# Sums of squares of the Mamba scan's grouped norm, with the ones as stationary side

## The chip, the cores and the metric

The kernel runs on one core of one Trainium2 chip. The metric is the time of one execution on the device, in microseconds (us). Before the change the median of three runs is 2793.15 us, from 2792.43 to 2793.49.

## The reference

The whole program is four transformer-like layers in a row on a tensor x of 2 x 1024 x 256 in f32. The change touches only the third layer's attention part, a Mamba block with 32 heads of 64, 8 groups and a state of 32. Its end is what matters here: the output y of the scan is gated, normed in 8 groups of 256 channels by the root of the mean of squares, and projected.

```python
states = lax.associative_scan(combine, (a, db), axis=1)[1]
y = jnp.einsum('blhps,blhs->blhp', states, Ch) + D_param[None, None, :, None] * x
y = y.reshape(Bb, Ll, D_SSM) * jax.nn.silu(z)
yg = y.reshape(Bb, Ll, G, D_SSM // G)
var = jnp.mean(yg * yg, axis=-1, keepdims=True)
y = (yg * lax.rsqrt(var + EPS)).reshape(Bb, Ll, D_SSM) * norm_w
return y @ W_out + b_out
```

## The kernel before

The program runs as stages on one core; each engine (TensorE, ACT, DVE, POOL and the SyncE queue) has its own ordered list of instructions, and semaphores tie them. The stage of the change is `MambaScan` (classes `Mamba` and `MambaSteps` hold its buffers and its preparation). It goes over 32 steps n: two batches of 1024 tokens, 8 groups g of four heads (256 channels), and two halves of 512 tokens (`c4`), so n = 16 b + 2 g + c4. Channels lie on partitions and tokens on columns; the 256 channels of a group are two tiles of 128 partitions.

What one step does, by the names of its pieces:
- "raw" (TensorE L1771, evicted by ACT L1893, first tap on POOL L2062), taps on DVE (L1967) and "silu" (ACT L1900) make the convolved input; each pair of steps needs two tiles of 1024 tokens, made ahead. Each tile takes two raw products of 512 columns.
- "scan" (TensorE L1784, DVE L1974), "xd" (transposes L1792, DVE L1981), "bd" (DVE L2002), "cb" (TensorE L1805, ACT L1913, DVE L2009, POOL L2076), "cp" (TensorE L1797, DVE L1995), "st" (TensorE L1824), "h" (DVE L2022), "within" (TensorE L1840) and "across" (TensorE L1857) are the chunked scan.
- "end" (DVE L2031, two of them) adds D x and takes y out of PSUM; "gate" (TensorE L1812, ACT L1920) makes silu(z), and POOL L2082 multiplies y by it, two tiles.
- "square" (ACT L1929, two, then POOL L2086) squares both tiles and adds them; "var" (TensorE L1864) sums over the partitions; "mean" (ACT L1935) adds eps to a 1/256 of it, and POOL L2090 raises it to the power -1/2.
- "out" (TensorE L1874, two halves r = 0, 1) multiplies y by W_out, ACT L1945 evicts it with that power as its scale, and POOL L2098 adds it to x.

In "var" each chunk of 128 tokens is the stationary side and two columns of ones the moving side, so the sums come out with tokens on partitions, one column (twice) for each of four chunks, 128 x 8 in all. That is the form in which ACT needs a scale for "out", whose rows are tokens.

The order of the pieces on each engine is written by hand. `AT` gives each kind of piece, for each engine, a place relative to n; `order` sorts all pieces by n plus place, and each engine works through its list strictly in that order. On POOL, "mean" of step n stands at n+1.42, ahead of "cb" of step n+2 (n+1.5) and of "gate" of step n+1 (n+1.55 and n+1.6). On TensorE, behind "var" of an odd n comes "across" of n+1 (n+1.6); behind that of an even n, up to 26, come two "raw" products (n+1.5) and then "across". Three of the odd steps (3, 11, 19) also have raw products there.

Each engine counts its pieces done in one semaphore (`self.products`, `self.activations`, `self.results`, `self.pooled`), so to wait for a piece is to wait for all ahead of it in that engine's list. POOL's raw piece also waits for the first "end" of the step whose input buffer it writes over, which for the tile made behind an even n is step n+1.

PSUM banks are dealt out in rings. Ring A has two banks and serves, in TensorE's order, "raw", "gate", "var" and "out"; `take` makes TensorE wait until ACT has done the piece that reads what the bank held last. For "var" that piece is "mean", for the others the eviction of the same name. ACT's "out" waits for POOL's "mean":

```python
w.wait_ge(self.products, self.pn[step])
w.wait_ge(self.pooled, self.gn["mean", n])
```

Of the kernel before, what the change touches and what calls it, by code (L numbers as in the profile page):

```python
# [1620 lines left out]
class MambaScan(Stage):  # L1621
# [8 lines left out]
    AT = {  # L1630
        "pe": {"raw": (-2.5, -2), "scan": (-1.1, -1, -0.8, -0.6), "xd": (-0.75, -0.6), "cp": (-0.2,),
             "cb": (-0.74,), "st": (0.05,), "within": (0.25,), "across": (0.6,), "gate": (0.15, 0.3), "var": (1.45,),
             "out": (1.85, 2.2)},
        "act": {"raw": (-2.45, -2), "silu": (-1.4, -1.2), "cb": (-0.5,), "gate": (0.15, 0.35),
             "square": (1.05, 1.1), "mean": (1.45,), "out": (1.95, 2.2)},
# [3 lines left out]
        "pool": {"raw": (-2.45, -2.2), "sel": (-1.1,), "cb": (-0.5,), "gate": (0.55, 0.6), "square": (1.15,),  # L1639
             "mean": (1.42,), "out": (1.85, 2.35)},  # L1640
    }


# [4 lines left out]
    def __init__(self, net, mem, norm, clear):  # L1648
        self.net, self.m, self.norm, self.clear = net, mem, norm, clear
        conv, half = self.conv, self.half = [], []  # L1650
        for q in range(4):
            t = (8 * q, .0) if q == 0 else (8 * q, -1.0)
            conv += [(t, q // 2, 16 + q % 2, 0), (t, q // 2, 18 + q % 2, 1)]
        for u in range(16):
            conv += [((2 * u, 0.0), u // 8, 2 * (u % 8) + s, s) for s in range(2)]
        p, a, d, g = [self.order(k) for k in ("pe", "act", "dve", "pool")]
        self.orders = {"pe": p, "act": a, "dve": d, "pool": g}
        self.raws = [s[1:3] for s in p if s[0] == "raw" and s[3] == 0]
        self.raw = {r: i for i, r in enumerate(self.raws)}
        beside = [k for kinds in self.NORM.values() for k in kinds]  # L1660
        self.pn, self.an, self.dn, self.gn = [{s: i + 1 for i, s in enumerate(s for s in o if s[0] not in beside)}
                                              for o in (p, a, d, g)]

        ring_a, ring_b = Slots(2), Slots(3)
        self.slot = {}
        for step in p:
            if step[0] in ("raw", "gate", "var", "out"):
                self.slot[step] = ring_a.take("a", ("mean", step[1]) if step[0] == "var" else step)
            elif step[0] in ("bt", "cb"):
                self.slot[step] = ring_b.take("a", step)  # L1670
            elif step[0] in ("scan", "xd", "cp"):
                self.slot[step] = ring_b.take("d", step)
        self.products = net.flag("m_products", len(self.pn))
        self.activations = net.flag("m_activations", len(self.an))
        self.results = net.flag("m_dve_results", len(self.dn))
        self.pooled = net.flag("m_pool_results", len(self.gn))
        self.crep = [net.flag("m_crep%d" % i, 64 * 16) for i in range(2)]
        self.blank = net.flag("m_blank", 1)
# [78 lines left out]
    def pe(self, e, w):  # L1757
# [3 lines left out]
        for step in self.orders["pe"]:  # L1761
# [81 lines left out]
            elif kind == "across":  # L1843
                w.wait_ge(self.results, self.dn["cp", n])
                w.wait_ge(self.results, self.dn["h", n, 2])
                for i in range(4):
                    c = 4 * c4 + i
                    if c == 0:
                        continue
                    o = slice(c * 128, c * 128 + 128)  # L1850
                    v = slice(i * 128, i * 128 + 128)
                    w.wait_ge(self.results, self.dn[("h", n, i - 1) if i else ("h", n - 1, 3)])
                    H = m.H[self.state(n, i - 1) % 4]
                    for h in range(4):
                        q = slice(32 * h, 32 * h + 32)
                        r = slice(64 * (h % 2), 64 * (h % 2) + 64)
                        t = e.matmul(net.PS[r, self.Y[h // 2], v], H[q, :], m.CP[q, o], start=False, stop=True,  # L1857
                                     skip_group_check=True)
                t.then_inc(P.sem, 1)
            elif kind == "var":  # L1860
                p = self.take(w, step, self.A)
                w.wait_ge(self.pooled, self.gn["square", n])
                for i in range(4):
                    t = e.matmul(p[:, 2 * i:2 * i + 2], m.sq[0][:, i * 128:i * 128 + 128], net.ones[:, 0:2], start=True,  # L1864
                                 stop=True)
                t.then_inc(P.sem, 1)
            elif kind == "out":
                p = self.take(w, step, self.A)
                w.wait_ge(self.pooled, self.gn["gate", n, 0])
                w.wait_ge(self.pooled, self.gn["gate", n, 1])  # L1870
                for j in range(2):
                    c = c4 * 512 + (2 * step[2] + j) * 128
                    for k in range(2):
                        t = e.matmul(p[:, j * 256:j * 256 + 256], m.Y[:, k, c:c + 128], m.Wout[:, 2 * g + k, :],  # L1874
                                     start=(k == 0), stop=(k == 1))
                t.then_inc(P.sem, 1)
            elif kind == "turn":
                w.wait_ge(self.results, self.dn["end", self.N - 1, 1])
                w.wait_ge(self.results, self.dn["h", self.N - 1, 2])
                self.norm.pe_turn(e, w, n)  # L1880

    def act(self, e, w):
        net, m, A = self.net, self.m, self.activations
        for step in self.orders["act"]:
# [37 lines left out]
            elif kind == "square":  # L1922
# [1 line left out]
                c4 = n % 2  # L1924
                w.wait_ge(self.pooled, self.gn["gate", n, s])
                if n > 0:
                    w.wait_ge(self.products, self.pn["var", n - 1])
                    w.wait_ge(self.pooled, self.gn["square", n - 1])
                e.activation(m.sq[s], m.Y[:, s, c4 * 512:c4 * 512 + 512], ACT.Square).then_inc(A.sem, 1)  # L1929
            elif kind == "mean":  # L1930
                w.wait_ge(self.products, self.pn["var", n])
                if n > 1:
                    w.wait_ge(A, self.an["out", n - 2, 0])
                    w.wait_ge(A, self.an["out", n - 2, 1])
                e.activation(m.rs[n % 2], self.bank(("var", n), self.A)[:, 0:8], ACT.Identity, scale=1.0 / 256.0,  # L1935
                             bias=net.eps).then_inc(A.sem, 1)
            elif kind == "out":
                r = step[2]
                p = self.bank(step, self.A)
# [3 lines left out]
                    w.wait_ge(self.pooled, self.gn["out", n - 1, r])  # L1943
                for j in range(2):
                    t = e.activation(m.O[r][:, j * 256:j * 256 + 256], p[:, j * 256:j * 256 + 256], ACT.Copy,  # L1945
                                     scale=m.rs[n % 2][:, 2 * (2 * r + j):2 * (2 * r + j) + 1])
                t.then_inc(A.sem, 1)
            elif kind == "xnt":
                self.wait_read(w)
# [93 lines left out]
    def pool(self, e, w):  # L2043
        net, m, G = self.net, self.m, self.pooled
        e.memset(m.RAW[:, :, 0:3], 0.0).then_inc(self.blank.sem, 1)
        for step in self.orders["pool"]:
# [40 lines left out]
            elif kind == "mean":  # L2087
                r = m.rs[n % 2]
                w.wait_ge(self.activations, self.an[step])
                e.tensor_tensor(r, r, m.mhalf, ALU.pow).then_inc(G.sem, 1)  # L2090
            elif kind == "out":
                b, g, c4 = self.where(n)
                i = b * 8 + c4 * 4 + 2 * step[2]
# [1047 lines left out]
```

## Time and profile before

| | |
|---|---|
| median of three runs | 2793.15 us |
| span of the profiled execution | 2813.6 us |
| instructions in the trace | 35158 |
| TensorE, busy in the span | 2635.8 us, 94% |
| DVE | 1672.5 us, 59% |
| ACT | 1069.7 us, 38% |
| POOL | 945.6 us, 34% |
| mean granted clock of TensorE | 0.968 |
| "var" products | 1884.7 to 2461.1 us, 256 passes |

The profile is of one execution. Its lines name a line of the kernel, an engine, an operation, the written and read tiles, shape and count, and in square brackets how long the engine stood idle before it and what released it. TensorE's time is given in two rows, PE for the products and PEld for the loads of the stationary side, which overlap. Products are pipelined and their ends are modelled, so the start of the next group tells better than the printed length how long a group held the engine. The granted clock is a share of TensorE's full speed: 1.00 is 2.4 GHz and 0.50 is 1.2 GHz.

### The profile page before, as it was taken

What the parts mean: (1) busy time and instruction counts of PE and PEld (TensorE: products, weight loads), DVE (VectorE), ACT (ScalarE), POOL (GpSimd) and SP (SyncE); (2) the same over time, 40 slices, a digit from 0 to 9 for tenths busy, and PEclk for the clock granted to TensorE, in tenths of its full rate; (3) what the DMA queues carried; (4) which work ended last, traced back from release to release, by engine and by line L of the source; (5) the groups of instructions that cost most, each with busy time, mean ns of one, the idle gap of its engine ahead of it and who ended that gap; (6) DMA issues with size and microseconds to landing.
All of it is one profiled execution on the core that took longest, in us unless ns stands there. A gap on an engine that the chain in (4) does not pass through costs nothing. (4 is left out here: it accounts for less than half of the span.)

```text
span 2813.6 us, 35158 instructions
## 1 busy us (share of the span) xinstructions
PE 2635.8 (94%) x13426; PEld 1672.0 (59%) x13426; DVE 1672.5 (59%) x3408; ACT 1069.7 (38%) x1954; POOL 945.6 (34%) x921
## 2 busy tenths in 40 slices
PE   7988989999999999999999997889999999967996
PEld 4445544564656655566565565646666666635896
DVE  6676671228576574665752325579888888743333
ACT  2534552114454443534543113434444444322222
POOL 3221210004232232322320005336766766751122
PEclk8999999999999999999999999989999999968998
DMA  5222111026000000000001000000000000070123
GB/s 187 61 61 69 54 46 61 0 73 76 1 1 1 1 1 1 1 1 1 16 1 71 33 0 30 1 20 12 16 16 12 16 12 16 9 287 25 57 72 133
DMA packets 57112, 109.11 MB, mean 39 GB/s; under 512 B 13792, under 2 KB 32480, under 8 KB 55792
## 3 DMA queue, kind: packets, MB, share of 16 engines
q1 hardware_dynamic: 53152, 96.47, 11.8%
q0 software_dynamic: 3792, 10.39, 1.0%
q8 instruction: 107, 1.75, 0.3%
q14 instruction: 61, 0.50, 0.1%
HBM read 71.16 MB, written 27.08 MB: 35 GB/s over the span
## 5 line engine op out<-in xcount | busy, mean ns | idle before, releaser
L1256 PE MATMUL ps<-back 128*128 128x512 f32 x576 | 292.0, 596 | 0.3 <-ACT back L1299 0.3
L1299 ACT ACTIVATE back<-ps 128x512 f32<-128x512 f32 x288 | 170.0, 597 | 266.3 <-PE ps L1247 264.6
L1294 ACT ACTIVATE back<-ps,front 128x128 f32<-128x128 f32 (+7 forms) x256 | 189.1, 739 | 71.6 <-DVE front L1345 69.6
L1388 POOL TENSOR_TENSOR back<-back 128x512 f32<-128x512 f32 x72 | 91.5, 1271 | 361.7 <-DVE back L1333 361.5
L1247 PEld LDWEIGHTS ps<-front,back 128*128 128x128 f32 x1152 | 140.8, 141 | 118.3 <-issue 95.0
L1398 POOL TENSOR_SCALAR back<-back,front 128x128 f32<-128x128 f32 (+5 forms) x192 | 143.0, 748 | 191.0 <-DVE front L1364 188.3
L809 ACT ACTIVATE back<-ps 128x1024 f32<-128x1024 f32 (+1 forms) x192 | 150.8, 811 | 128.1 <-PE ps L721 127.6
L1345 DVE TENSOR_REDUCE front<-ps 128x1 f32<-128x128 f32 (+7 forms) x256 | 194.0, 758 | 8.8
L1974 DVE TENSOR_TENSOR_SCAN back<-ps,back 128x512 f32<-128x512 f32 x128 | 155.7, 1217 | 50.4 <-PE ps L1784 49.8
L1338 DVE TENSOR_TENSOR ps<-ps,front 128x128 f32<-128x128 f32 x256 | 76.0, 297 | 166.0 <-PE ps L1238 166.0
L1247 PE MATMUL ps<-front,back 128*128 128x128 f32 x1152 | 170.5, 273 | 3.3 <-DVE back L1370 3.3
L697 PE MATMUL ps<-rounded 128*128 128x512 f32 (+3 forms) x384 | 141.0, 410 | 12.8 <-DMA rounded<-kh 4.7
L1228 PE MATMUL ps<-front 128*128 128x512 f32 x320 | 152.1, 598 | 0.0
L1771 PE MATMUL ps<-front 128*128 128x512 f32 x320 | 148.8, 610 | 1.9 <-ACT back L1893 1.0
L1238 PE MATMUL ps<-front,back 128*128 128x512 f32 (+3 forms) x384 | 145.5, 490 | 3.4 <-POOL back L1388 3.4
L857 DVE CUSTOM_DVE_ANT_0 ps<-ps,back 128x128 f32<-128x128 f32 (+3 forms) x256 | 120.8, 513 | 44.9 <-PE ps L697 43.5
L931 POOL TENSOR_SCALAR_AFFINE_SELECT back<-back 128x256 f32<-128x256 f32 x128 | 51.8, 408 | 278.6 <-ACT back L809 278.2
L1238 PE MATMUL ps<-back 128*128 128x512 f32 (+3 forms) x384 | 145.0, 486 | 0.0
L320 POOL TENSOR_TENSOR back<-back,front 128x4 f32<-128x4 f32 x8 | 8.1, 1015 | 385.6 <-DVE back L302 385.6
L389 ACT ACTIVATE back<-ps 128x512 f32<-128x512 f32 x64 | 38.2, 597 | 256.1 <-PE ps L360 256.0
L402 DVE TENSOR_TENSOR back<-back,ps 128x512 f32<-128x512 f32 x64 | 44.0, 687 | 151.7 <-PE ps L365 143.4
L1812 PE MATMUL ps<-front 128*128 128x512 f32 x256 | 128.8, 626 | 0.0
(319 smaller groups left out, 5697.5 us busy)
## 6 DMA issues: line engine op xcount, KB each, us to landing
whole<-l_w SPq DMA_DIRECT2D x32, 512.0 KB
front<-back SPq DMA_DIRECT2D x128, 64.0 KB, 2.0
rounded<-qh SPq DMA_DIRECT2D x28, 256.0 KB
rounded<-kh SPq DMA_DIRECT2D x56, 128.0 KB
front<-xg SPq DMA_DIRECT2D x47, 129.0 KB
xg<-front SPq DMA_DIRECT2D x2, 3008.0 KB, 37.0
front<-l_win SPq DMA_DIRECT2D x1, 4640.0 KB, 17.7
front<-l_wgu SPq DMA_DIRECT2D x2, 2048.0 KB, 13.5
```

The lines of the kernel that those rows point to most:

```text
L697: t = e.matmul(o[:, 0:n], self.QS[:, s, h, qt], self.KS[:, s, h, 512 * r:512 * r + n], start=True, stop=True)
L809: e.activation(self.PT[j % 2][:, 2 * a:2 * a + 2, c:512], PS[:, 2 * a:2 * a + 2, c:512], ACT.Exp).then_inc(A.sem, 1)
L1228: t = e.matmul(o, W, XNT[:, k, tok], start=(k == 0), stop=(k == 1))
L1238: t = e.matmul(s[:, c:c + m], self.Q[:, h, qt * 128:qt * 128 + 128], self.Kt[G % 2][:, c:c + m], start=True, stop=True)
L1247: t = e.transpose(p[:, h * 128:h * 128 + 128], self.P[n % 2][:, h, j * 128:j * 128 + 128], net.ident)
L1256: e.matmul(PS[:, 7, :], self.V[:, j, G % 4 * 128:G % 4 * 128 + 128], self.turned(("turn", n, j)), start=(j == 0), stop=(j == qt)).then_inc ...
L1294: e.activation(self.P[n % 2][:, h, :nk], s[:, :nk], ACT.Exp, bias=st[:, 0, h:h + 1], scale=1.0, accum_out=st[:, 1, h:h + 1]).then_inc(A.se ...
L1299: e.activation(self.turned(step), self.bank(step), ACT.Copy).then_inc(A.sem, 1)
L1345: e.tensor_reduce(self.st[n % 2][:, 0, h:h + 1], s[:, :nk], AX.X, ALU.max, negate=True).then_inc(D.sem, 1)
L1398: e.tensor_scalar(self.P[n % 2][:, h, :nk], self.P[n % 2][:, h, :nk], self.st[n % 2][:, 3, h:h + 1], 1.0, ALU.mult, ALU.mult).then_inc(S.s ...
L1771: t = e.matmul(p, m.Win[:, k, col:col + 128], XNT[:, k, tok], start=(k == 0), stop=(k == 1))
L1974: e.tensor_tensor_scan(m.LT[:, h, four, :].rearrange("p a b -> p (a b)"), self.bank(step, self.B), m.ident4, 0.0, ALU.mult, ALU.add).then_ ...
```

## The change

The ones become the stationary side, 32 columns of them, and each chunk of squares the moving side. The four chunks' results go to the four groups of 32 partitions of one bank, so that each product uses another column tile of the array; the sums then lie along the columns, each 32 times over on partitions. A new ACT piece "spread" copies that 128 x 128 block to SBUF with the 1/256 and eps, a new TensorE piece "flip" transposes it into a bank of its own from ring A, and "mean" on ACT now copies every 32nd column, four in all. POOL's power works on four columns instead of eight. Places: "flip" n+1.6 on TensorE, "spread" n+1.48 and "mean" n+1.62 on ACT, "mean" n+1.62 on POOL. The bank of "var" is now free after "spread", and that of "flip" after "mean".

```diff
--- before.py
+++ after.py
@@ -1630,14 +1630,14 @@
     AT = {
         "pe": {"raw": (-2.5, -2), "scan": (-1.1, -1, -0.8, -0.6), "xd": (-0.75, -0.6), "cp": (-0.2,),
              "cb": (-0.74,), "st": (0.05,), "within": (0.25,), "across": (0.6,), "gate": (0.15, 0.3), "var": (1.45,),
-             "out": (1.85, 2.2)},
+             "flip": (1.6,), "out": (1.85, 2.2)},
         "act": {"raw": (-2.45, -2), "silu": (-1.4, -1.2), "cb": (-0.5,), "gate": (0.15, 0.35),
-             "square": (1.05, 1.1), "mean": (1.45,), "out": (1.95, 2.2)},
+             "square": (1.05, 1.1), "spread": (1.48,), "mean": (1.62,), "out": (1.95, 2.2)},
         "dve": {"tap1": (-1.8, -1.7), "tap2": (-1.8, -1.5), "tap3": (-1.8, -1.4),
              "scan": (-1, -0.8, -0.65, -0.5), "xd": (-0.65, -0.4), "cp": (-0.25,), "bd": (-0.4,), "cb": (-0.4,),
              "h": (0.2, 0.3, 0.3, 0.5), "end": (0.65, 0.7)},
         "pool": {"raw": (-2.45, -2.2), "sel": (-1.1,), "cb": (-0.5,), "gate": (0.55, 0.6), "square": (1.15,),
-             "mean": (1.42,), "out": (1.85, 2.35)},
+             "mean": (1.62,), "out": (1.85, 2.35)},
     }
 
 
@@ -1664,8 +1664,8 @@
         ring_a, ring_b = Slots(2), Slots(3)
         self.slot = {}
         for step in p:
-            if step[0] in ("raw", "gate", "var", "out"):
-                self.slot[step] = ring_a.take("a", ("mean", step[1]) if step[0] == "var" else step)
+            if step[0] in ("raw", "gate", "var", "flip", "out"):
+                self.slot[step] = ring_a.take("a", {"var": ("spread", step[1]), "flip": ("mean", step[1])}.get(step[0], step))
             elif step[0] in ("bt", "cb"):
                 self.slot[step] = ring_b.take("a", step)
             elif step[0] in ("scan", "xd", "cp"):
@@ -1861,9 +1861,13 @@
                 p = self.take(w, step, self.A)
                 w.wait_ge(self.pooled, self.gn["square", n])
                 for i in range(4):
-                    t = e.matmul(p[:, 2 * i:2 * i + 2], m.sq[0][:, i * 128:i * 128 + 128], net.ones[:, 0:2], start=True,
-                                 stop=True)
+                    t = e.matmul(p[32 * i:32 * i + 32, 0:128], net.ones[:, 0:32], m.sq[0][:, i * 128:i * 128 + 128],
+                                 start=True, stop=True)
                 t.then_inc(P.sem, 1)
+            elif kind == "flip":
+                p = self.take(w, step, self.A)
+                w.wait_ge(self.activations, self.an["spread", n])
+                e.transpose(p[:, 0:128], m.sq[1][:, 0:128], ident).then_inc(P.sem, 1)
             elif kind == "out":
                 p = self.take(w, step, self.A)
                 w.wait_ge(self.pooled, self.gn["gate", n, 0])
@@ -1924,16 +1928,21 @@
                 c4 = n % 2
                 w.wait_ge(self.pooled, self.gn["gate", n, s])
                 if n > 0:
-                    w.wait_ge(self.products, self.pn["var", n - 1])
+                    w.wait_ge(self.products, self.pn["flip", n - 1])
                     w.wait_ge(self.pooled, self.gn["square", n - 1])
                 e.activation(m.sq[s], m.Y[:, s, c4 * 512:c4 * 512 + 512], ACT.Square).then_inc(A.sem, 1)
+            elif kind == "spread":
+                w.wait_ge(self.products, self.pn["var", n])
+                w.wait_ge(self.pooled, self.gn["square", n])
+                e.activation(m.sq[1][:, 0:128], self.bank(("var", n), self.A)[:, 0:128], ACT.Identity,
+                             scale=1.0 / 256.0, bias=net.eps).then_inc(A.sem, 1)
             elif kind == "mean":
-                w.wait_ge(self.products, self.pn["var", n])
+                w.wait_ge(self.products, self.pn["flip", n])
                 if n > 1:
                     w.wait_ge(A, self.an["out", n - 2, 0])
                     w.wait_ge(A, self.an["out", n - 2, 1])
-                e.activation(m.rs[n % 2], self.bank(("var", n), self.A)[:, 0:8], ACT.Identity, scale=1.0 / 256.0,
-                             bias=net.eps).then_inc(A.sem, 1)
+                e.activation(m.rs[n % 2][:, 0:4], self.bank(("flip", n), self.A)[:, 0:128:32],
+                             ACT.Copy).then_inc(A.sem, 1)
             elif kind == "out":
                 r = step[2]
                 p = self.bank(step, self.A)
@@ -1943,7 +1952,7 @@
                     w.wait_ge(self.pooled, self.gn["out", n - 1, r])
                 for j in range(2):
                     t = e.activation(m.O[r][:, j * 256:j * 256 + 256], p[:, j * 256:j * 256 + 256], ACT.Copy,
-                                     scale=m.rs[n % 2][:, 2 * (2 * r + j):2 * (2 * r + j) + 1])
+                                     scale=m.rs[n % 2][:, 2 * r + j:2 * r + j + 1])
                 t.then_inc(A.sem, 1)
             elif kind == "xnt":
                 self.wait_read(w)
@@ -2087,7 +2096,7 @@
             elif kind == "mean":
                 r = m.rs[n % 2]
                 w.wait_ge(self.activations, self.an[step])
-                e.tensor_tensor(r, r, m.mhalf, ALU.pow).then_inc(G.sem, 1)
+                e.tensor_tensor(r[:, 0:4], r[:, 0:4], m.mhalf[:, 0:4], ALU.pow).then_inc(G.sem, 1)
             elif kind == "out":
                 b, g, c4 = self.where(n)
                 i = b * 8 + c4 * 4 + 2 * step[2]
```

## Rows read from the trace of the kernel before

**Rows 1.** The page: busy time of each engine, its share of the span, instructions.

```profile
PE 2635.8 (94%) x13426; PEld 1672.0 (59%) x13426; DVE 1672.5 (59%) x3408; ACT 1069.7 (38%) x1954; POOL 945.6 (34%) x921
```

**Rows 2.** Table by stretch: busy us (instructions) by engine, granted clock, DMA share, GB/s.

```profile
1900.00:2440.00 540.00, 539.54 (x4293) 362.39 (x4291) 471.96 (x559) 230.88 (x388) 375.73 (x247) 1.00 0.06 14
```

**Rows 3.** Timeline, TensorE, around odd n: start, length in us, work, idle before.

```profile
2139.72 0.66 PE L1792 MATMUL ps<-front,back 128*128 128x128 f32 x4
2140.31 1.15 PE L1805 MATMUL ps<-back 32*128 32x128 f32 x8
...
2143.45 0.60 PE L1792 MATMUL ps<-front,back 128*128 128x128 f32 x4
2143.88 0.95 PE L1864 MATMUL ps<-front 128*128 128x2 f32 x8
2144.76 0.89 PE L1857 MATMUL ps<-back 32*64 32x128 f32 x24
...
2146.02 1.89 PE L1874 MATMUL ps<-front,back 128*128 128x256 f32 x8
...
2150.59 1.89 PE L1874 MATMUL ps<-front,back 128*128 128x256 f32 x8
```

**Rows 4.** Timeline, TensorE, around the even n that follows.

```profile
2158.70 0.95 PE L1864 MATMUL ps<-front 128*128 128x2 f32 x8
2159.51 3.68 PE L1771 MATMUL ps<-front 128*128 128x512 f32 x8
2163.12 1.10 PE L1857 MATMUL ps<-back 32*64 32x128 f32 x32
...
2166.45 3.60 PE L1771 MATMUL ps<-front 128*128 128x512 f32 x8
```

**Rows 5.** Timeline, the earlier product in four column tiles, its copy and transposes.

```profile
1719.21 1.92 PE L1505 MATMUL ps<-front 128*32 128x512 f32 x16
...
1721.20 0.60 ACT L1525 ACTIVATE front<-ps 128x512 f32<-128x512 f32 x1 [1.67 <-PE ps L1505]
...
1721.85 0.66 PE L1510 MATMUL ps<-front 128*128 128x128 f32 x4 [0.72 <-ACT front L1525]
```

**Rows 6.** Timeline, ACT, DVE and POOL, same stretch as rows 3.

```profile
2144.87 0.27 ACT L1935 ACTIVATE back<-ps,front 128x8 f32<-128x8 f32 x1 [0.68 <-PE ps L1864]
...
2146.57 0.68 DVE L2002 TENSOR_TENSOR back<-back 128x512 f32<-128x512 f32 x1
...
2147.53 2.64 POOL L2076 TENSOR_TENSOR back<-back,front 128x512 f32<-128x512 f32 x1
...
2147.95 0.84 ACT L1945 ACTIVATE front<-ps,back 128x256 f32<-128x256 f32 x2 [0.24 <-PE ps L1874]
...
2148.96 1.40 DVE L2031 SCALAR_TENSOR_TENSOR back<-back,front,ps 128x512 f32<-128x512 f32 x2
...
2150.13 2.50 POOL L2082 TENSOR_TENSOR back<-back 128x512 f32<-128x512 f32 x2
```

**Rows 7.** Instructions of two lines: POOL's powers of 8 and of 4 columns.

```profile
L2090 POOL TENSOR_TENSOR back<-back x32: 1647/2002/2339, 1886.7 to 2461.8; 128x8 f32<-128x8 f32 x32
...
L320 POOL TENSOR_TENSOR back<-back,front x8: 1007/1008/1048, 503.3 to 1707.1; 128x4 f32<-128x4 f32 x8
```

**Rows 8.** Timeline, POOL, same stretch as rows 4.

```profile
2165.23 1.12 POOL L2062 TENSOR_SCALAR back<-back,front 128x1024 f32<-128x1024 f32 x1 [1.45 <-DVE back L2031]
2166.32 2.51 POOL L2082 TENSOR_TENSOR back<-back 128x512 f32<-128x512 f32 x2
```

**Rows 9.** Two idle gaps of TensorE, and the table by stretch behind each.

```profile
647.71 2.50 PE L1238 MATMUL ps<-front,back 128*128 128x128 f32 x6 [2.42 <-POOL back L1388]
...
1873.99 0.49 PE L1784 MATMUL ps<-rounded 128*128 128x512 f32 x1 [3.52 <-DVE back L1995]
...
648.00:653.00 5.00, 5.00 (x10) 2.89 (x10) 3.22 (x15) 1.48 (x6) 0.95 (x3) 0.50 1.21 194
1876.00:1886.00 10.00, 10.00 (x40) 6.84 (x37) 4.34 (x7) 1.30 (x2) 1.27 (x1) 0.51 0.07 16
```

## The prediction, made before the change was run

> **What bounds the kernel now.** I read the page's busy shares first: TensorE holds 94% of the span [rows 1]. Then the table by stretch: between 1900 and 2440 us, which is the Mamba scan, TensorE is busy 539.54 of 540 us at a granted clock of 1.00, while DVE has 471.96, ACT 230.88 and POOL 375.73 [rows 2]. So in this stage an instruction taken from or added to TensorE counts in full, and so does every wait that its queue meets; what the other engines do counts only through such a wait. Then I read the timeline of single steps on each engine. A step is one of the 32 values of n. Two kinds alternate: behind an odd n the next thing on TensorE is "across" (143.88 to 144.76; here and below 2000 us are left off such times) [rows 3]; behind an even n two "raw" products stand between [rows 4].
>
> **TensorE's own work.** Each 512-column chunk has four products for its sums of squares. They are f32 and run in two passes, so eight passes with a 128-column load each. They hold the engine 0.88 us behind odd n (143.88 to 144.76) [rows 3] and 0.81 behind even n (158.70 to 159.51) [rows 4]. After the change there are again eight passes, now 128 columns long through 32 loaded columns, in four column tiles. The trace has that shape once: 16 passes of 512 columns in four column tiles took 1.92 us [rows 5], so 0.03 us for 128 columns; and 24 passes of 128 columns in smaller tiles took 0.89, so 0.037 each [rows 3]. I take 8 x 0.037 = 0.30 us, with 0.24 below and the old 0.88 above. A change of tile shape also costs: four full transposes take 0.43 us up to the next full product (143.45 to 143.88), but 0.59 where the next work is tiled (139.72 to 140.31) [rows 3], so 0.16 us. The new turn ("flip") is one more transpose, 0.43 / 4 to 0.59 / 4; I take 0.13.
>
> Behind an even n: 0.30 + 0.16 + 0.13 = 0.59 against 0.81, a gain of 0.22. The two raw products hide the copy ("spread"), and the turn comes 3 us later.
>
> Behind an odd n nothing lies between the new product and its turn (places 1.45 and 1.6 in the list; raw stands between only for three of the odd steps). So TensorE's queue stands still for the copy. From the end of a product's slot to ACT's start are 0.11 us (144.76 to 144.87) [rows 3, 6]; the copy of 128 columns lies between 0.27 for 8 columns [rows 6] and 0.60 for 512 [rows 5], I take 0.35; from ACT's end to the turn 0.05 (1721.80 to 1721.85) [rows 5]. Sum 0.51, and the step is 0.30 + 0.16 + 0.51 + 0.13 = 1.10 against 0.88, a loss of 0.22. Over 16 steps of each kind the two cancel: on TensorE's own queue the swap is worth about 0 us, between -9 and +22 us by the bounds.
>
> Here the rows show a cost for going from full to tiled work, 0.16 us. The Trainium skill's page "TensorEngine Tiling (Array Packing)", section Key Properties, says that "changing tiling mode (not just tile) drains the TensorE"; the trace agrees on the way in. Behind even n the new product stands between two full-array products, so by that rule it pays twice, which would turn the gain of 0.22 into 0.06 and add 16 x 0.16 = 2.6 us. No row separates the way out.
>
> **What moves on POOL, and who waits for it.** This is the large term. The power on POOL shrinks from 8 to 4 columns: 2.00 us to 1.01, by the row of an existing 4-column power [rows 7]. That is no gain by itself, since POOL has slack. But its place goes from n+1.42 to n+1.62. Before, it stood ahead of "cb" of n+2 (n+1.5) and of the two "gate" products of n+1 (n+1.55 and n+1.6). Now it stands behind them. The gates need DVE's "end" of n+1, which needs "across" of n+1, which TensorE issues after the turn. And ACT's "out" of n (its scale is the power's result) waits for the power; ACT's "out" frees a bank of the two-bank ring A, and with the turn's slot added the ring works out so: behind odd n, product "out" (n,1) takes the bank of "out" (n,0); behind even n, the second "raw" of the next pair does. Before, ACT evicted "out" (n,0) 0.04 us after the end of the product (147.91 to 147.95) [rows 3, 6], since the power was long done. Now TensorE's queue waits for across, end, two gates, power, eviction, and everything queued behind it waits too. Worked out:
>
> Odd n: DVE's "bd" ends at 147.25, POOL's cb starts at 147.3 instead of 147.53 and takes 2.64, to 149.9; the gates 2.50, to 152.4; the power 1.0, to 153.4; ACT's two evictions 0.84, to 154.25; TensorE at 154.3 [rows 6, 7]. DVE's "end" runs from 148.96 to 150.36 and fits in. The product came at 150.59 [rows 3]. Delay 3.7 us, flip's loss included, since that chain hangs on an earlier TensorE product and not on the turn.
>
> Even n: across starts at 163.12; POOL's raw step, which waits for the first "end", starts at 165.23, the gates at 166.32 and end at 168.83 [rows 4, 8]. Then power 1.0, evictions 0.05 + 0.84, TensorE 0.05: the bank is free 7.65 us after across starts. TensorE reaches the second raw at 166.45 + 1.72 = 168.17 (the two products take 3.60 with a tail of 0.17; half of the rest is one), that is 5.05 us after across. Stall 2.6 us; less the 0.22 gained, delay 2.4.
>
> There are 12 plain odd steps, 3 odd and 14 even steps with raw (taken alike), one even step without (taken at 2.8 us), and at the end the squares of n = 31 queue on ACT behind such an eviction, some 3 us. 12 x 3.7 + 17 x 2.4 + 2.8 + 3 = 91 us. Bounds: if POOL's cb and raw steps and DVE cost nothing, across to release is 1.1 + 0.7 + 2 x 1.25 + 1.0 + 0.9 = 6.2 to 6.4 us, so stalls of 0.5 (odd, against 5.83) and 1.3 (even), 30 us in all; above, 22 us more if the tiles don't overlap.
>
> **The clock.** These stalls are gaps of about 3.2 us (odd) and 2.4 us (even) in which TensorE does nothing. Where the trace has such gaps the clock fell: after a gap of 2.42 us the stretch 648 to 653 ran at 0.50, after one of 3.52 us the stretch 1876 to 1886 at 0.51, each with TensorE busy throughout [rows 9]; that is the level of 1.2 GHz. Half speed for 5 to 10 us costs 2.5 to 5 us of work. I take 4.3 us for each of the 13 long gaps and, since shorter gaps may not all do it, 3.4 us for half of the 17 shorter ones: 56 + 29 = 85 us. From nothing to 30 x 5 = 150 us is the range of this term.
>
> **Sum.** 91 + 85 = 176 us, all inside the scan. The profiled execution spans 2813.6 us, 20.5 above the median of 2793.15 (0.7%); its stage times are used as they are, and the sum goes on the median: 2793 + 176 = 2969 us.
>
> **The rivals.**
> 1. The stalls come but the clock holds: they are in a stage that is otherwise dense, unlike the gap at 1874, before which TensorE had been loose. Then 2793 + 91 = 2884 us, 2840 to 2915 with the bounds. For it: the stretch 1900 to 2440 never left 1.00. Against it: it never had a gap.
> 2. The eviction isn't what TensorE meets: the bank is free in time, because DVE and POOL run ahead once TensorE is slower. It decides where across-to-release falls under 5.05 us; it stands at 7.65 and its shortest form at 6.2. Then only the swap is left, and if four tiles overlap fully, the switch costs nothing and the copy takes 0.27, each step gains: (0.81 - 0.24 - 0.11) x 16 + (0.88 - 0.24 - 0.43 - 0.11) x 16 = 9 us, 2784 us, faster. This is the case on the other side.
> 3. The stall is there but mostly given back, by POOL's shorter power and by queues that catch up in it: 2793 + 30 = 2823 us.
> 4. The change doesn't do what it says: the four column tiles run one after the other, 8 x 0.107 = 0.86 us (a full transposes' pace of 0.43 / 4). Then 16 us more on any case; it alone decides nothing.
>
> **How the numbers follow.** Stalls and falling clock 0.58 (2915 to 3050); stalls alone 0.29; mostly given back 0.05; near nothing 0.02; faster 0.06. The likeliest gives 2969. The range 2855 to 3045 holds nearly all of the first and most of the second. A measurement of this kernel tells about 0.2% from no change: faster 0.06, same 0.02, slower 0.92.
>
> **What would show it.** In the profile after: POOL's power at about 1.0 us, right behind the second gate; ACT's "out" idle for POOL, some 3 us behind the product instead of 0.04; TensorE idle until ACT's "out" at the second "out" product and the second "raw", about 30 times, 3.2 and 2.4 us; a granted clock under 1.00 in the scan; TensorE idle about 0.5 us until the copy behind odd n; the new product's eight passes in 0.3 us. I am wrong if TensorE stays at 99% busy there (rival 2), if the clock stays 1.00 (rival 1), or if a second chain, such as DVE's taps, takes over the wait.

## The result

The changed kernel takes 2939.41 us (median of 4, 2936.02 to 2947.74) against 2792.79 of the kernel before on the same chip: 1.054 times as long, 95% interval 1.0522 to 1.0559. That is 146.6 us slower; 176 was forecast. A second measurement on another chip gave 1.055.

The page of the changed kernel: busy time of each engine, and the granted clock in 40 slices.

```profile
PE 2680.5 (91%) x13458; PEld 1674.9 (57%) x13458; DVE 1662.8 (56%) x3408; ACT 1071.8 (36%) x1986; POOL 922.8 (31%) x921
...
PEclk8989999999999999999999998899998999888998
```

TensorE is at 91% where it had 94% [rows 1], and the clock row has eights in slices 31, 35 and 36, which lie in the scan. The table by stretch for the scan, from the first "var" product to the last, first of the changed kernel, then of the kernel before (columns as in [rows 2]):

```profile
1889.80:2618.40 728.60, 614.57 (x4599) 385.64 (x4601) 487.77 (x591) 246.79 (x446) 380.47 (x266) 0.93 0.05 11
```

```profile
1884.70:2461.10 576.40, 573.36 (x4572) 385.81 (x4572) 498.48 (x590) 245.21 (x415) 402.94 (x266) 1.00 0.06 14
```

The stretch went from 576.4 to 728.6 us. TensorE stood idle for 3.0 us of it before and for 114.0 now, and was busy 41 us longer at a mean clock of 0.93. DVE and ACT were busy for nearly the same time in both, POOL for 22 us less. So the loss is in this stage. It is 152 us, while the two profiled spans (2813.6 and 2946.0) differ by only 132: ahead of the scan the changed kernel's execution took 5 us more, and behind it 25 us less. Most of those 25 us is one wait in the last stage, which the execution of the kernel before met and the other did not. What it waited for the profile does not show ("issue"):

```profile
2545.08 0.69 PE L2735 MATMUL ps<-front 128*128 128x128 f32 x2 [15.86 <-issue]
```

The sums below are therefore made on the scan stage, and the medians for the whole.

### The profile page after: what moved, and what is told of

It reads as the page before. It is cut to its first block and busy times, and to the rows that moved or that the text cites. A ratio compares the mean times of both kernels' runs of the same rounds, so it can differ in the third digit from the quotient of the medians.

```text
span 2946.0 us, 35302 instructions
## 1 busy us (share of the span) xinstructions
PE 2680.5 (91%) x13458; PEld 1674.9 (57%) x13458; DVE 1662.8 (56%) x3408; ACT 1071.8 (36%) x1986; POOL 922.8 (31%) x921
## 5 line engine op out<-in xcount | busy, mean ns | idle before, releaser
L1299 ACT ACTIVATE back<-ps 128x512 f32<-128x512 f32 x288 | 170.0, 597 | 266.2 <-PE ps L1247 264.5
L1771 PE MATMUL ps<-front 128*128 128x512 f32 x320 | 166.3, 659 | 58.7 <-ACT front L1954 56.9
L1247 PEld LDWEIGHTS ps<-front,back 128*128 128x128 f32 x1152 | 140.8, 141 | 118.4 <-issue 95.0
L1878 PE MATMUL ps<-front,back 128*128 128x256 f32 x512 | 139.8, 423 | 44.2 <-ACT front L1954 44.2
L2085 POOL TENSOR_TENSOR back<-back,front 128x512 f32<-128x512 f32 x32 | 88.8, 2776 | 238.4 <-DVE back L2011 238.4
L1228 PE MATMUL ps<-front 128*128 128x512 f32 x320 | 152.1, 598 | 0.0
L1878 PEld LDWEIGHTS ps<-front,back 128*128 128x128 f32 x512 | 106.6, 211 | 78.7 <-ACT front L1954 54.9
L1954 ACT ACTIVATE front<-ps,back 128x256 f32<-128x256 f32 x128 | 53.7, 471 | 233.7 <-POOL back L2099 193.3
```

What stands on the lines that cost most here:

```text
L1228: t = e.matmul(o, W, XNT[:, k, tok], start=(k == 0), stop=(k == 1))
L1247: t = e.transpose(p[:, h * 128:h * 128 + 128], self.P[n % 2][:, h, j * 128:j * 128 + 128], net.ident)
L1299: e.activation(self.turned(step), self.bank(step), ACT.Copy).then_inc(A.sem, 1)
L1771: t = e.matmul(p, m.Win[:, k, col:col + 128], XNT[:, k, tok], start=(k == 0), stop=(k == 1))
```

## The profile after: two waits, thirty times

TensorE around an odd n in the changed kernel, which answers to [rows 3]; "flip" is L1870, "out" L1878:

```profile
2262.12 0.43 PE L1864 MATMUL ps<-front 128*32 128x128 f32 x8
2263.12 0.30 PE L1870 MATMUL ps<-front 128*128 128x128 f32 x1 [0.58 <-ACT front L1937]
2263.35 0.88 PE L1857 MATMUL ps<-back 32*64 32x128 f32 x24
...
2264.51 1.89 PE L1878 MATMUL ps<-front,back 128*128 128x256 f32 x8
...
2267.26 1.98 PE L1812 MATMUL ps<-front 128*128 128x512 f32 x4
2272.72 1.54 PE L1878 MATMUL ps<-front,back 128*128 128x256 f32 x3 [3.47 <-ACT front L1954]
```

ACT, DVE and POOL in the same stretch, which answers to [rows 6]; L1937 is "spread", L2085 POOL's "cb", L2091 the gates, L2099 the power and L1954 ACT's "out":

```profile
2262.61 0.37 ACT L1937 ACTIVATE front<-ps,front 128x128 f32<-128x128 f32 x1 [0.28 <-PE ps L1864]
...
2264.71 0.68 DVE L2011 TENSOR_TENSOR back<-back 128x512 f32<-128x512 f32 x1
...
2265.53 2.77 POOL L2085 TENSOR_TENSOR back<-back,front 128x512 f32<-128x512 f32 x1 [7.51 <-DVE back L2011]
...
2268.27 2.48 POOL L2091 TENSOR_TENSOR back<-back 128x512 f32<-128x512 f32 x2
...
2270.72 1.01 POOL L2099 TENSOR_TENSOR back<-back 128x4 f32<-128x4 f32 x1
...
2271.82 0.84 ACT L1954 ACTIVATE front<-ps,back 128x256 f32<-128x256 f32 x2 [6.22 <-POOL back L2099]
```

POOL's cb starts 0.14 us after DVE's bd has ended, the gates follow, then the power, then ACT's evictions, and TensorE's second "out" at 2272.72, after 3.47 us of nothing. The first "out" had been done since 2266.40 (2264.51 + 1.89), so its result lay in its bank for 5.4 us before ACT could scale it.

The same around an even n, TensorE first, which answers to [rows 4]; then DVE, POOL and ACT, which answer to [rows 8]:

```profile
2429.81 3.70 PE L1771 MATMUL ps<-front 128*128 128x512 f32 x8
2433.35 0.27 PE L1870 MATMUL ps<-front 128*128 128x128 f32 x1
2433.55 1.10 PE L1857 MATMUL ps<-back 32*64 32x128 f32 x32
...
2436.88 1.88 PE L1771 MATMUL ps<-front 128*128 128x512 f32 x4
2442.18 1.13 PE L1771 MATMUL ps<-front 128*128 128x512 f32 x2 [3.43 <-ACT front L1954]
```

```profile
2436.75 2.49 POOL L2091 TENSOR_TENSOR back<-back 128x512 f32<-128x512 f32 x2
...
2438.22 4.74 DVE L1976 SCALAR_TENSOR_TENSOR back<-back,front 128x1024 f32<-128x1024 f32 x3
2439.20 2.00 POOL L2099 TENSOR_TENSOR back<-back 128x4 f32<-128x4 f32 x1
2441.29 0.84 ACT L1954 ACTIVATE front<-ps,back 128x256 f32<-128x256 f32 x2 [6.90 <-POOL back L2099]
```

Here the second raw product of the pair waits, 3.43 us. The power took 2.00 us, not 1.0: it started while the first of the three taps was running on DVE (L1976, 4.74 us for three). In the single instructions that tap ends 1.12 us behind the power's start, and the power 0.88 us after the tap. The tap itself had started beside POOL's gates and took 2.11 us, where the middle one of its kind takes 1.28. The list of waits of TensorE in the scan (us in total, times, longest):

```profile
PE ps L1771 <- ACT front L1954: 56.9, 17, 3.7
PE ps L1878 <- ACT front L1954: 44.2, 13, 4.4
PE ps L1870 <- ACT front L1937: 8.4, 14, 0.9
PE ps L1864 <- POOL front L2095: 4.6, 1, 4.6
```

And the clock behind the gap that ended at 2442.18:

```profile
2437.00:2442.00 5.00, 1.76 (x5) 0.45 (x3) 4.85 (x4) 0.71 (x2) 4.20 (x3) 1.00 0.22 52
2444.00:2447.00 3.00, 3.00 (x35) 1.34 (x34) 0.83 (x2) 1.81 (x3) 1.35 (x2) 0.51 0.00 0
2448.00:2460.00 12.00, 11.42 (x104) 8.27 (x103) 8.66 (x12) 5.39 (x9) 3.57 (x4) 1.00 0.00 1
```

TensorE idles from 2438.8 to 2442.2; from 2444 to 2447 it runs at 0.51, that is the level of 1.2 GHz, and from 2448 at 1.00 again. In the trace's record of the clock this happened 22 times in the scan, for 3.4 us (16 times) or 6.8 us (6 times), 96 us together.

## Experiments

Each is one or a few edits to the changed kernel or to the kernel before. They ran on chips on which the kernel before took 2787 to 2789 us and, for one set of four, 2816 us; so I compare ratios to the kernel before on the same chip. "On the scale of the expectation" means the ratio times 2792.79 us.

### The power ahead of the gates

```diff
-             "mean": (1.62,), "out": (1.85, 2.35)},
+             "mean": (1.52,), "out": (1.85, 2.35)},
```

> The changed kernel with one place altered: POOL's power (mean) stands at n+1.52, ahead of the two gate products of n+1 instead of behind them. Theory (the power's place makes the stalls): the some 30 gaps of 3.4 us before the second out and the second raw product go, the clock stays at 1.00 in the scan, and the time falls by some 150 us to 2775 to 2805 us, within 10 us of the kernel before (TensorE's own queue: 0.22 us gained behind even n, 0.22 lost behind odd n). Rival (the two extra TensorE steps and the extra bank of ring A make the loss): the time stays above 2900 us and the gaps stay.

Measured: 2804.33 us, ratio 1.0050 (1.0037 to 1.0064). One place in POOL's list gives back nine tenths of the loss. There is no gap at the raw products any more, the power takes 1.0 us throughout, and the clock in the scan never falls. All else of the change (tiled products, copy, turn, third user of ring A between "var" and "out") is still there, so the rival is out. It isn't all the way, though, 15.6 us over the kernel before where I expected at most 10: 12 gaps, most of them of 1.0 us, stay at the second "out" behind odd n. Rows of one (DVE's bd, POOL's cb, the power, ACT's out, TensorE's second out):

```profile
2352.42 0.68 DVE L2011 TENSOR_TENSOR back<-back 128x512 f32<-128x512 f32 x1
...
2353.25 2.78 POOL L2085 TENSOR_TENSOR back<-back,front 128x512 f32<-128x512 f32 x1 [6.44 <-DVE back L2011]
...
2355.99 1.01 POOL L2099 TENSOR_TENSOR back<-back 128x4 f32<-128x4 f32 x1
...
2357.09 0.84 ACT L1954 ACTIVATE front<-ps,back 128x256 f32<-128x256 f32 x2 [3.78 <-POOL back L2099]
...
2357.98 1.99 PE L1878 MATMUL ps<-front,back 128*128 128x256 f32 x8 [1.03 <-ACT front L1954]
```

The power now waits in POOL's list for cb, which waits for DVE's bd; in the kernel before it was done ahead of cb.

### The old products with the late power

```diff
-             "mean": (1.42,), "out": (1.85, 2.35)},
+             "mean": (1.62,), "out": (1.85, 2.35)},
```

This is the kernel before, with nothing of the change but the place.

> The kernel before with one place altered: POOL's power, still of 8 columns and without the new products, stands at n+1.62 behind the gate products of n+1. Theory: gaps before the same two TensorE products, longer by up to 1 us than with 4 columns: 17 x 3.7 + 13 x 4.4 + 3 = 123 us, and 40 to 60 us more through the clock: 2955 to 2985 us. Rival (the new products or their bank make the loss): within 10 us of 2793.

Measured: 2987.66 us, ratio 1.0716 (1.0699 to 1.0733). Moving one instruction of 2 us, which nothing had waited for, cost 199 us; on the scale of the expectation that is 2993 us, 8 above its top. Its table by stretch in the scan:

```profile
1900.00:2550.00 650.00, 545.45 (x3831) 352.22 (x3830) 418.94 (x503) 207.48 (x351) 334.03 (x223) 0.90 0.04 11
```

TensorE is idle for 104.6 of these 650 us at a mean clock of 0.90. The gaps stand at the same two products, 17 of 66.6 us and 13 of 57.0 us together. The two experiments agree from both sides: the place makes the loss, with either form of the products.

### The power between the gates

```diff
-             "mean": (1.62,), "out": (1.85, 2.35)},
+             "mean": (1.58,), "out": (1.85, 2.35)},
```

> The changed kernel with POOL's power at n+1.58, between the two gate products of n+1: the chain to the bank's release is one POOL product of 1.25 us shorter. Theory: the 30 gaps shrink from 3.45 us to about 2.2 us, 37 us off, and with shorter gaps the clock falls less often, 20 to 45 us off more: 2857 to 2882 us. Rival (the clock falls after gaps of this length as before): only the 37 us, 2902 us.

Measured: 2875.59 us on the chip where the kernel before takes 2815.54, ratio 1.0212 (1.0197 to 1.0228), which is 2852 us on the scale of the expectation. The waits, and the power by form (busy us, mean ns):

```profile
PE ps L1878 <- ACT front L1954: 28.3, 13, 3.2
PE ps L1771 <- ACT front L1954: 20.4, 17, 1.5
...
L2099 POOL TENSOR_TENSOR back<-back 128x4 f32<-128x4 f32 x32 | 32.8, 1024 | 1.5 <-ACT back L1944 1.5
```

For comparison the same row of the changed kernel:

```profile
L2099 POOL TENSOR_TENSOR back<-back 128x4 f32<-128x4 f32 x32 | 48.4, 1514 | 2.7 <-ACT back L1944 2.7
```

The odd gaps are 28.3 / 13 = 2.2 us as expected, but the even ones 20.4 / 17 = 1.2 us. POOL and DVE in one even step of this run:

```profile
2020.79 1.02 POOL L2099 TENSOR_TENSOR back<-back 128x4 f32<-128x4 f32 x1
2021.02 3.46 DVE L1976 SCALAR_TENSOR_TENSOR back<-back,front 128x1024 f32<-128x1024 f32 x2
```

The power still has a tap beside it, for 0.8 to 1.0 of its 1.02 us in all 16 such steps, but it starts up to 0.24 us ahead of the tap and no longer inside it, and it is not slowed. So a gate less is worth about 1.25 us in each step, and a power that starts ahead of the tap another 1.0 us in those. The clock fell behind 4 of the 30 gaps, for 14 us in all and only behind odd ones, where in the changed kernel it fell 22 times for 96 us. The gaps are 52 us shorter in all, where I gave 37, and 82 us less at half clock are 35 us at the 0.43 measured below, within the 20 to 45 I gave. Together 87 us, which explains the 5 us under the expectation.

### The power of eight columns again

```diff
-                e.activation(m.rs[n % 2][:, 0:4], self.bank(("flip", n), self.A)[:, 0:128:32],
+                e.activation(m.rs[n % 2], self.bank(("flip", n), self.A)[:, 0:128:16],
...
-                e.tensor_tensor(r[:, 0:4], r[:, 0:4], m.mhalf[:, 0:4], ALU.pow).then_inc(G.sem, 1)
+                e.tensor_tensor(r, r, m.mhalf, ALU.pow).then_inc(G.sem, 1)
```

> The changed kernel with the power, in its late place, again of 8 columns (each value twice). Theory: what POOL's power takes longer is added to every gap, 0.65 to 1 us behind odd n and at most that behind even n where it runs beside DVE's taps: 15 to 30 us in the gaps, and 10 to 25 us more through the clock: 2964 to 2994 us. Rival (the power's length is hidden): 2939 us. Against the late power with the old products, 2988 us, it tells what the new products add or save when the gaps stand: equal within 15 us by my sum.

Measured: 3008.42 us where the kernel before takes 2815.54, ratio 1.0688 (1.0672 to 1.0705), 2985 us on the scale of the expectation and inside it. The gaps grew from 101.1 to 119.8 us in all and the time at half clock from 96 to 147 us. The power takes 1.64 us behind odd n and 2.63 where it starts inside a tap, 0.63 more than with four columns in both, and the mean gap grew by 18.7 / 30 = 0.62: the power's length counts in full once it is in the chain. Against the old products with the late power (1.0716, 1.0699 to 1.0733) the two intervals overlap: the halved power apart, the swap itself costs nothing that these runs can tell.

### Work put into the gaps

```diff
         i, before = self.slot[key]
         if before:
             engine, freed = before
+            if freed[0] == "out" and freed[2] == 0 and freed[1] < 30:
+                w.wait_ge(self.results, self.dn["end", min(freed[1] + 1, 31), 1])
+                for _ in range(8):
+                    self.pe_engine.matmul(self.net.PS[:, 5, 0:256], self.m.Wout[:, 0, 0:128], self.m.Wout[:, 1, :],
+                                          start=True, stop=True)
...
+        self.pe_engine = e
```

Before a product that will wait for the bank of a first "out", TensorE waits for DVE's "end" of the step behind and then computes the unread products.

> The changed kernel with work put into the gaps: before each of the 30 products that wait for the first out's bank, TensorE computes eight f32 products of 256 columns into a bank that is free then (16 passes of 0.215 us, 3.4 us), whose result nobody reads. The chain to the bank's release is unchanged. If the fallen clock costs its share beside the gaps: the clock stays at 1.00 from 1900 us to the end of the scan and the time falls by about half of the 96 us at half clock, to 2885 to 2900 us. If the clock costs nothing of its own (what is slow at half clock is hidden in the next gap): 2939 us or a little more.

Measured: 2906.01 us, ratio 1.0419 (1.0401 to 1.0438). An even step of it (L1751 the unread products, L1777 the raw one), and its table by stretch:

```profile
2265.96 3.62 PE L1751 MATMUL ps<-front 128*128 128x256 f32 x16
2269.41 1.88 PE L1777 MATMUL ps<-front 128*128 128x512 f32 x4
...
1900.00:2500.00 600.00, 591.93 (x4390) 396.49 (x4390) 439.23 (x518) 218.36 (x389) 329.60 (x229) 1.00 0.05 12
```

TensorE does 103 us more work than the changed kernel, none of it useful, and the kernel is 33 us faster, since the clock stays at 1.00. That is less than I expected. In the steps with raw products hardly a gap was left (0.7 us over 4 times in all), so the filling could itself have been too long; the next run leaves room.

### The same with three quarters of the filling

```diff
-                for _ in range(8):
+                for _ in range(6):
```

> As the kernel with the filled gaps, but six unread products instead of eight before each of the 30 waiting ones: 12 passes of 0.215 us, 2.6 of the 3.6 us, so that the chain to the bank still ends last everywhere and the filling itself can't lengthen a step. If the half clock costs 45 to 55 us of its own in the changed kernel: the clock stays at 1.00, gaps of 0.8 to 1.0 us stay, and the time is 45 to 55 us below that of the changed kernel on the same chip. If the 34 us of the kernel with eight products were all: 30 to 36 us below.

> The changed kernel once more, beside the one with partly filled gaps on the same chip: 1.054 times the kernel before, gaps of 3.45 us and 90 to 105 us at half clock in the scan.

Measured on one chip: 2902.82 us, ratio 1.0410 (1.0391 to 1.0429), and for the changed kernel again 2937.34 us, ratio 1.0550 (1.0529 to 1.0571). Tables by stretch, first partly filled, then the changed kernel:

```profile
1900.00:2500.00 600.00, 571.91 (x4285) 377.39 (x4285) 438.84 (x518) 217.81 (x389) 329.66 (x229) 1.00 0.05 12
```

```profile
1900.00:2500.00 600.00, 508.07 (x3795) 317.37 (x3792) 415.56 (x498) 208.44 (x371) 313.82 (x218) 0.95 0.05 12
```

Gaps of 0.8 to 0.9 us stay, so the chain still ends last, and the time hardly moved against the full filling. The half clock is worth 34.5 us by the medians. The two profiled executions agree: from the first "var" to the last they take 688.7 and 721.5 us, 32.8 apart, with 3 and 79 us at half clock, so 0.43 us for each. My 45 to 55 was wrong, the lower alternative right. I had counted half of the time at half clock, but part of that time falls where TensorE would have idled anyway: in the first profile of the changed kernel the six falls of 6.8 us begin 1.1 to 1.6 us before the gap ends, 8 of the 96 us.

### The turn behind across

```diff
-             "flip": (1.6,), "out": (1.85, 2.2)},
+             "flip": (1.65,), "out": (1.85, 2.2)},
...
-             "square": (1.05, 1.1), "spread": (1.48,), "mean": (1.62,), "out": (1.95, 2.2)},
+             "square": (1.05, 1.1), "spread": (1.48,), "mean": (1.7,), "out": (1.95, 2.2)},
```

On top of the power ahead of the gates.

> As the kernel with the early power, and the turn (flip) also moved from n+1.6 to n+1.65 on TensorE, behind across of n+1, with ACT's mean from n+1.62 to n+1.7. The copy is then hidden behind odd n as well. Theory: TensorE's wait for the copy (20.1 us over 28 times in the changed kernel) goes, against the kernel with the early power alone 8 to 12 us (0.6 us in each plain odd step), so 2765 to 2795 us and faster than the kernel before by some 10 us. Rival (POOL's power then waits for the later turn and delays the gates and the next squares, so TensorE meets a new wait): no gain or a loss against the early power alone.

Measured: 2808.14 us, ratio 1.0074 (1.0060 to 1.0088): no gain, a miss. The waits of TensorE for the copy are gone, and the other row has grown by what they were:

```profile
PE ps L1878 <- ACT front L1954: 21.7, 13, 3.3
```

It was 13.5 us over 12 times with the early power alone. The second "out" is released by the power, which hangs on bd and cb and not on the turn. So TensorE came 0.6 us earlier and waited 0.6 us longer. A wait is free where a later one follows on the same engine whose release doesn't hang on the first.

### Both waits gone

On top of that, ACT's mean at n+1.58, and POOL's power in the plain odd steps back where the kernel before has it:

```diff
                 for r, x in enumerate(places):
+                    if kind == "mean" and engine == "pool" and n % 2 and n not in (3, 11, 19):
+                        x = 1.42
+                    if kind == "mean" and engine == "act" and n == 31:
+                        x = 1.7
```

> The new products with all their waits taken off TensorE's queue: the turn behind across (n+1.65), ACT's mean at n+1.58, POOL's power at n+1.52 behind cb where raw products stand between, and at n+1.42 ahead of cb in the plain odd steps, where the early power of the first experiment still left gaps of 1.0 us. Theory: no gap of over 0.3 us in the scan but the last; TensorE's own saving is left, 0.22 us behind even n and 0.29 to 0.35 behind odd n, 9 us in all: 2774 to 2786 us, faster than the kernel before by 0.2 to 0.5%. Rival (changes of tile shape or the 32 more transposes eat the saving): 2786 to 2795 us.

Measured: 2808.43 us (10 runs) against 2815.54, ratio 0.9979 (0.9967 to 0.9991): faster than the kernel before by 0.21%, 2787 us on the scale of the expectation. That is 1 us above its upper end and inside the range of the rival, so the time alone doesn't decide between the two. What TensorE still waits for in the scan:

```profile
PE ps L1868 <- POOL front L2099: 3.2, 1, 3.2
...
PE ps L1882 <- ACT front L1958: 0.3, 1, 0.3
```

From the second to the 28th "var" it took 495.2 us, the kernel before 502.4: 7.2 us in 26 steps, 0.28 us a step, and nearly the same behind even and odd n (22.02 to 21.74 and 14.82 to 14.52 us from one "var" to the next). The sum for TensorE alone (0.22 even, 0.29 to 0.35 odd) holds, and nothing has eaten the saving.

### The turn right behind the product, nothing else in the way

The same with "flip" at 1.6 as in the change, and without the two lines for n = 31.

> The same, but with the turn back at n+1.6, right behind the new product in the plain odd steps. Theory: TensorE waits 0.58 us for the copy in each of 14 steps as in the changed kernel and nowhere else, so 6 to 8 us more than with the turn behind across: 2781 to 2793 us, about the kernel before. Rival (the wait is hidden by what it lets the other engines catch up): the same time as with the turn behind across.

Measured: 2816.69 us (11 runs), ratio 1.0005 (0.9992 to 1.0017). The same stretch took 501.9 us, the only wait in it is

```profile
PE ps L1872 <- ACT front L1939: 8.4, 14, 0.9
```

and it costs 6.7 us, 12 times 0.56. So with the places of the change on TensorE and no late power the swap is worth nothing, as forecast; with the turn put behind across it is worth 0.2% (0.1 to 0.3).

## The prediction, step by step

**TensorE's own work.** Right in its net, a little off behind odd n. The eight tiled passes plus the change of shape hold the engine 0.46 us (0.10 more before them, 0.36 after), against 0.30 + 0.16. The wait for the copy is 0.58 us against 0.51, and the last run shows the net of zero directly (+0.6 us from the first "var" to the last, without the late power). Step by step it gains 0.23 us behind even n (22.02 to 21.79), forecast 0.22, and loses 0.35 behind plain odd n (14.82 to 15.17), forecast 0.22; the three odd steps with raw products gain like the even ones, which brings the net back to zero. A second cost of 0.16 us behind even n, for the way back to full-array work, would have left 0.06 us of the gain there; it doesn't show. The fourth rival, tiles one after the other, is out.

**Who waits for the power.** Right in mechanism, place and count: 13 gaps at the second "out" and 17 at the second raw product. The odd term was forecast at 3.7 us, of which 3.2 a gap; the gaps are 44.2 / 13 = 3.4 us. The even term was mis-sized: 2.4 us forecast, 56.9 / 17 = 3.3 measured. The step that failed is "power 1.0". I took the length of a 4-column power from rows where DVE did nothing like the taps [rows 7]; [rows 8] show the stretch, but I did not ask what DVE does in it. Where the power starts while a tap is running it takes 2.00 us, in 16 of the 17. In the other one DVE had other work (norm statistics), the power took 1.03 us and the gap was 2.46 us, the number forecast. The traces give it a simple form: in every run where a power starts inside a tap, it ends a fixed time after that tap's end, 0.88 us with four columns and 1.51 with eight, whatever was left of the tap (0.28 to 1.17 us). One power of the run with both waits gone started inside "bd", which also reads two tiles in SBUF, with 0.29 us of it left, and took 1.16 us. The kernel before has it too: its power took 2.33 us in the 16 steps in which it started 0.83 us before a tap's end and 1.65 in the others, and that is the spread of [rows 7], which I read as one number. So DVE's taps did enter the chain, the third sign of being wrong. The Trainium skill's page "GPSIMD Engine Reference", section Specifications, says that POOL's SBUF interfaces are shared with VectorE, with contention for DVE instructions "with two SBUF inputs"; the taps have two, and the trace agrees where the power starts inside a tap. The power between the gates shows that lying beside one is not enough: started first, it took 1.02 us. With the 2.00 us the sum would have been 16 us larger.

**The clock.** It fell, as forecast and unlike the first rival, after 22 of 30 gaps; forecast were 13 + 17 / 2, about as many. The term was 85 us; with 0.43 us for each of 96 us it is 41. Two figures in it failed. I took 5 to 10 us at half speed for each fall from the two stretches of [rows 9], where the falls here last 3.4 us and at most 6.8, 4.3 in the mean; and I took half of the time as loss.

**The sum.** Between the first and the last "var" the changed kernel takes 728.3 us, the kernel before 574.6: 153.7 more. Gaps at the two products 101.1, what of each stall lies ahead of the gap as the profile draws it (the modelled tail of a product, 0.17 us, 30 times) 5, half clock 41, the last squares 2, the swap with its wait for the copy 0.6: 150, and 4 us stay without a name. Forecast were 91 and 85. Both errors are of size and of opposite sign: the stalls came out 18 us larger, the clock 44 us smaller, and what is left between forecast and measurement is 29 us. That they partly cancelled is luck: with the clock term right alone the forecast would have been 2925 us, and with the stalls right alone 2987.

**The rivals.** The range given for the first rival, 2840 to 2915 us, doesn't follow from the bounds it names, which make 2823 to 2906; nothing hung on it. That the bank is free in time was excluded by the shortest form of the chain, 6.2 us against 5.05, and the trace has it at 8.6 us behind even n (2433.55 to 2442.18). Nor were the stalls given back: all 30 gaps stand. The reason I see is that DVE, ACT and POOL are fed by TensorE's across in the same step, so each step starts the chain anew.

What stays open: why gaps of the same length (3.4 to 3.6 us are found on both sides) make the clock fall 22 times and not the other 8, and why it lasts once 3.4 and once 6.8 us. No run here was made for it.

## What to carry to other kernels

In engines with strict lists, the cost of moving an instruction is not its length but what stands between its old and its new place, followed to the next reader of the buffer that it releases: one power of 1 to 2 us, moved behind two products that wait for a later step, cost up to 199 us. Before a step is added to a ring of two banks, write down for each product whose eviction it will wait for, and what that eviction waits for on the other engines. When a new instruction has to wait on an engine that is the bound, first see whether a later wait stands on it whose release doesn't hang on the first: then the first is free, and to remove it alone gains nothing. And where the length of an instruction varies in a trace, as 1.65 to 2.34 us in [rows 7], find out what the neighbouring engine was doing at its start before you take one number for it.

## What the runs showed of the hardware

- A power of 4 columns on POOL takes 1.01 us and one of 8 columns 1.65. Started while a tap with two SBUF inputs is running on DVE, it ends 0.88 and 1.51 us after the tap, so 2.00 us and 2.33 to 2.66 here; started 0.04 to 0.24 us ahead of the tap it takes 1.02 us.
- Gaps of mostly 3.4 us on TensorE in otherwise dense work let the clock fall to 0.50 for 3.4 or 6.8 us about three times in four, and a microsecond at half clock cost 0.43 us. Behind 17 gaps of mostly 1.2 us it never fell, behind 13 of mostly 2.25 us it fell 4 times.
- Useless products in such gaps made the kernel 1.1 to 1.2% faster than idling did.
- Four f32 products of 128 columns in four column tiles hold the engine 0.36 us, and coming to them from full-array work costs 0.10 us.
